# Output and down products with their weights held in the array and 512 tokens streaming, their results turned back into rows through VectorE and memory

## The reference

```python
x = x + _layernorm(attn(_layernorm(x)))      # 16 heads of 128, causal softmax, b_Q b_K b_V b_O
    out = jnp.einsum('bqhe,hed->bqd', z, W_O) + b_O
x = x + _layernorm(mlp(_layernorm(x)))       # 4-bit weights with block scales, 2048 wide
    gelu = jnp.tanh(0.7978845608028654 * (gate + 0.044715 * gate ** 3)) * gate * 0.5 + gate * 0.5
    inter = gelu * up
    out = jnp.einsum('tn,hn->th', inter, Wd)
```

## Time and profile before

| | |
|---|---|
| median of 3 runs | 1584.81 us (1583.91 to 1586.49) |
| the profiled execution, its own time | 1591.08 us |
| its span, first to last instruction | 1588.4 us |
| PE busy / weight loads | 1561.3 us (98%) / 1397.9 us (88%) |
| DVE, ACT, POOL busy | 1061.5 (67%), 974.1 (61%), 712.5 us (45%) |
| matmuls recorded | 9600 |
| granted TensorE clock, mean | 0.998 |
| DMA: bytes moved, mean rate | 167.69 MB, 106 GB/s |

### The profile page before, as it was taken

How to read it: one execution, slowest core, us unless ns; L and a number is a source line. 1 busy time by engine, 2 the same in 40 slices (tenths; PEclk the granted TensorE clock), 3 DMA queues, 4 the chain that set the end, 5 groups by cost and what they waited for, 6 DMA issues and landing times.

```text
span 1588.4 us, 28430 instructions
## 1 busy us (share of the span) xinstructions
PE 1561.3 (98%) x9600; PEld 1397.9 (88%) x9600; DVE 1061.5 (67%) x3074; ACT 974.1 (61%) x2433; POOL 712.5 (45%) x1069
## 2 busy tenths in 40 slices
PE   7999999999999999999999999999999999999998
PEld 5889898988998899889899989898888888888887
DVE  4656677677677777777767766666656565565665
ACT  5887677667776676767776767644444444444443
POOL 4674454545554455444554544333333333333333
PEclk9999999999999999999999999999999999999999
DMA  4554434443444344444443454471000011000000
GB/s 118 178 174 122 140 116 139 149 138 124 143 148 138 123 144 131 140 130 131 149 143 117 142 163 136 155 278 41 27 14 27 14 32 36 14 28 14 27 14 27
DMA packets 157440, 167.69 MB, mean 106 GB/s; under 512 B 15856, under 2 KB 130672, under 8 KB 157296
## 3 DMA queue, kind: packets, MB, share of 16 engines
q1 hardware_dynamic: 157296, 165.89, 32.9%
HBM read 94.53 MB, written 71.30 MB: 104 GB/s over the span
## 4 chain that ended last, share of the span: by engine, by line
PE 79%; DMA 6%; ACT 6%; DVE 5%; SPq 3%; issue 1%; POOL 1%; DVEq 0%; POOLq 0%
PE fbank L700 13%; PE fbank L701 13%; PE fbank L702 13%; PE obank L702 6%; PE obank L701 6%; PE obank L700 6%; PE ubank L700 5%; PE ubank L702 5%; PE ubank L701 5%; DMA turned_scratch<-turned 3%; PE ubank L724 3%; PE fbank L802 2%; DMA back<-turned_scratch 2%; SPq L498 2%; ACT probs L597 1%
## 5 line engine op out<-in xcount | busy, mean ns | idle before, releaser
L700 PE MATMUL fbank<-xnT_hi,wqk_hi 128*128 128x512 f32 x768 | 302.9, 394 | 3.7 <-POOL wqk_lo L1215 2.7
L701 PE MATMUL fbank<-xnT_lo,wqk_hi 128*128 128x512 f32 x768 | 301.3, 392 | 0.0
L702 PE MATMUL fbank<-xnT_hi,wqk_lo 128*128 128x512 f32 x768 | 300.7, 392 | 0.0
L1246 POOL TENSOR_TENSOR pT_lo<-back,pT_hi 128x512 fp32r<-128x512 f32 x128 | 166.1, 1298 | 274.3 <-ACT pT_hi L662 274.3
L608 ACT ACTIVATE w_raw<-fbank 128x512 f32<-128x512 f32 x128 | 76.5, 598 | 254.3 <-PE fbank L702 254.3
L1208 POOL TENSOR_SCALAR probs<-probs,rsum 128x128 f32<-128x128 f32 (+1 forms) x512 | 209.2, 428 | 20.7 <-DVE rsum L901 17.7
L702 PEld LDWEIGHTS fbank<-xnT_hi,wqk_lo 128*128 128x128 f32 x768 | 145.1, 189 | 31.8
L893 DVE CUSTOM_DVE_ANT_0 probs<-ubank,mask 128x128 f32<-128x128 f32 (+1 forms) x512 | 154.9, 355 | 26.4 <-PE ubank L702 26.1
L700 PEld LDWEIGHTS fbank<-xnT_hi,wqk_hi 128*128 128x128 f32 x768 | 145.2, 189 | 27.6 <-issue 2.9
L701 PEld LDWEIGHTS fbank<-xnT_lo,wqk_hi 128*128 128x128 f32 x768 | 145.3, 189 | 22.5
L982 DVE SCALAR_TENSOR_TENSOR w_raw<-w_raw,fbank 128x512 f32<-128x512 f32 x128 | 88.0, 687 | 104.0 <-ACT w_raw L608 102.2
(11 more groups left out here) (124 smaller groups left out, 4566.1 us busy)
## 6 DMA issues: line engine op xcount, KB each, us to landing
turned_scratch<-turned SPq DMA_DIRECT2D x128, 384.0 KB, 2.6
back<-turned_scratch SPq DMA_DIRECT2D x512, 96.0 KB, 2.2
w_raw<-in_w_pairs SPq DMA_DIRECT2D x32, 256.0 KB, 3.3
w_hi_scratch<-w_hi SPq DMA_DIRECT2D x48, 128.0 KB, 2.0
w_lo_scratch<-w SPq DMA_DIRECT2D x48, 128.0 KB, 2.0
x_res<-in_x SPq DMA_DIRECT2D x16, 256.0 KB, 2.9
wqk_hi<-w_hi_scratch SPq DMA_DIRECT2D x16, 256.0 KB, 4.6
wqk_lo<-w_lo_scratch SPq DMA_DIRECT2D x16, 256.0 KB, 5.0
```

The lines of the kernel that those rows point to most:

```text
L700: nc.tensor.matmul(out, a[0], b[0], start=start, stop=False, skip_group_check=skip)
L701: nc.tensor.matmul(out, a[0], b[1], start=False, stop=False, skip_group_check=skip)
L702: return nc.tensor.matmul(out, a[1], b[0], start=False, stop=stop, skip_group_check=skip)
L1246: pool.tensor_tensor(lo[:].rearrange("p u b (a j) -> p (u b) a j", j=32), mem.back[m % 2][:, :, 0:2].rearrange("p a u b j -> p (u b) a j") ...
```

## The change

The output product of a head, and the down product of a tile in MLP chunks 0 to 6, are now six matmuls of 512 columns in place of twelve of 256: 128 output columns of the weights are held, and the 512 tokens stream. The result has output columns in the partitions and tokens along the row. The down product of chunk 7 stays as it was.

To get rows again: ACT copies the result to `given` (a view of `stream`), with `b_O` as its bias in the attention, where DVE did this before (in the MLP ACT did it before too). DVE transposes it in blocks of 32, two instructions of 128x512 a chunk (`turn_given` on DVE). SP writes 512 KB to memory, waits until they have landed, and reads them back in four DMAs of 128 KB (`turn_given` on SP). Statistics and standardising (`given_stats`, `given_standard`) read the result there; `given_stats` waits for the four reads. This is done 15 times: 8 in place of the attention's results, 7 in place of the MLP's. In the attention the two transposes stand at the "sum" of steps 3 and 4, the DMAs after the `fetch` of step 5, the statistics at the "sum" of steps 6 and 8 (all at the end of step 5 before). In MLP chunk 0 the transposes stand after `gated` of tile 4, the statistics after that of tile 5, and POOL's roots move from before to after `inter_lo` of tile 4; in later chunks the transposes come at step 0, the statistics at step 2 (steps 0 and 1 before), and everything behind them one step later. `b_O` is loaded as two columns instead of a row broadcast to all partitions.

```diff
-X1_ROOTS, NEXT_ROOTS = 6, 13
+X1_ROOTS, NEXT_ROOTS = 9, 13
...
+        backs = sb("back", [P, 2, 4, 3, 2, 32])
+        self.back = [backs[:, i] for i in range(2)]
...
+        self.given = self.stream[:].rearrange("p (h a) d -> p h (a d)", h=2)
+        places = [raw, backs[:].rearrange("p n a u b j -> p (n a u b j)")[:, 0:TT * D]]
+        self.given_turned = [v.rearrange("p (a t h j) -> p a t h j", t=TT, h=2, j=BLK)
+                             for v in places]
...
+    def turn_given(n):
+
+        view = mem.given_turned[0 if n < NCH - 1 else 1]
+        sp.wait_ge(s.given, 2 * n + 2)
+        if n:
+            sp.wait_ge(s.given_back, 64 * n)
+        sp.dma_start(given_v.rearrange("k i a c -> (k i) a c"),
+                     view.rearrange("p a t h j -> p a (t h j)")).then_inc(s.given_sent, 16)
+        sp.wait_ge(s.given_sent, 16 * (n + 1))
+        for a in range(4):
+            sp.dma_start(view[32 * a:32 * a + 32].rearrange("p k t h j -> p k (t h j)"),
+                         given_v[:, :, a].rearrange("k i c -> i k c")).then_inc(s.given_back, 16)
...
         fetch(n)
+        if c and j == 5:
+            turn_given(c - 1)
...
+        turn_given(NCH - 1 + c)
         finish_y(c)
...
+        elif kind == "out" and h == HEADS - 1:
+            act.wait_ge(s.out, m // HEADS + 1)
+            for i in range(2):
+                last = act.activation(mem.given[:, i], mem.columns[i], ACT.Identity,
+                                      bias=mem.bias_o[:, i:i + 1])
+            last.then_inc(s.out_used, 1)
...
-            for t in range(TT):
-                last = three(mem.obank[t // 2][:, t % 2, :],
-                             [p[:, t * P:(t + 1) * P] for p in mem.zT],
-                             [p[:, h, :] for p in mem.wo_p],
-                             h == 0 and t % 2 == 0, h == HEADS - 1, skip=True)
+            for i in range(2):
+                last = three(mem.columns[i], [p[:, h, i * P:(i + 1) * P] for p in mem.wo_p],
+                             [p[:] for p in mem.zT], h == 0, h == HEADS - 1, skip=True)
...
+            for i in range(2) if c < NCH - 1 else ():
+                last = three(mem.columns[i], [mem.w4_at(p, k)[:, i, m % 2, :] for p in range(2)],
+                             [p for p in mem.iT[m % 4]], m == 0, m == NT - 1, skip=True)
+
+            for t in range(TT) if c == NCH - 1 else ():
...
+    def turn_given(n, i):
...
+        dve.transpose(view[:, :, :, i, :].rearrange("p a t j -> p t a j"),
+                      mem.given[:, i].rearrange("p (t a i) -> p t a i", t=TT, i=BLK)
+                      ).then_inc(s.given, 1)
+
+    def given_stats(n, t):
+        dve.wait_ge(s.given_back, 64 * (n + 1))
...
-    X1_AT = {(5, "end"): (0, 1, 2), (9, "end"): (3, 4, 5, 6)}
+    X1_AT = {(3, "sum"): (-2,), (4, "sum"): (-1,), (6, "sum"): (0,), (8, "sum"): (1, 2),
+             (9, "end"): (3, 4, 5, 6)}
...
-                last = dve.tensor_tensor(xn[:, 2 * i:2 * i + 2, :], mem.obank[i][:],
-                                         mem.bias_o[:].unsqueeze(1).broadcast_to([P, 2, D]),
-                                         ALU.add)
...
+        if c == 0:
+            for part in {4: (-1,), 5: (0, 1), 6: (2,), 7: (3,), 8: (4,), 9: (5,)}.get(m, ()):
+                finish_y(part, c)
+        else:
+            for part in {0: (-1,), 2: (0, 1), 3: (2,), 4: (3,), 5: (4,), 6: (5,)}.get(j, ()):
+                finish_y(part, c)
...
-            if m == (4 if c == 0 else 3):
+            if m == (5 if c == 0 else 4):
                 roots(y_norm(c))
```

More of the change, by code:

```diff
@@ L273, in __init__ @@
         self.obank = [bank(f"obank{i}", [P, 2, D]) for i in range(2)]
+        self.columns = [b[:].rearrange("p a d -> p (a d)") for b in self.obank]
         self.gbank = [*(self.fbank[GATES[i] % FB] for i in range(2)), self.fbank[bank_of(LAST_Z)]]
@@ L631, in scalar_program @@
         full(nth(key), mem.xnT[0][:, kt, SEQ:], mem.fbank[bank_of(key)][:, 0:SEQ]).then_inc(s.hi, 1)
-    act.wait_ge(s.bias, 64)
+    act.wait_ge(s.bias, 80)
     weights_hi(2)
@@ L692, in scalar_program @@
             for i in range(2):
-                ins = act.activation(mem.stream[:, 2 * i:2 * i + 2, :], mem.obank[i][:], ACT.Copy)
+                ins = act.activation(mem.given[:, i], mem.columns[i], ACT.Copy)
             ins.then_inc(s.down_used, 1)
@@ L918, in standardise, with given_standard @@
         return last
-    def finish_x1(part, c):
-        if part in (0, 1):
-            stats_of(xn, 2 * part)
+    def turn_given(n, i):
+        view = mem.given_turned[0 if n < NCH - 1 else 1]
+        if i == 0 and n == 0:
+            dve.wait_ge(s.w_split, len(PAIRS))
+        dve.transpose(view[:, :, :, i, :].rearrange("p a t j -> p t a j"),
[3 more added lines that the diff above has]
+        dve.wait_ge(s.given_back, 64 * (n + 1))
+        view = mem.given_turned[0 if n < NCH - 1 else 1]
+        for i in (t, t + 1):
+            last = dve.bn_stats(mem.stats[:, i, :], view[:, :, i].rearrange("p k h j -> p k (h j)"))
+        after(last)
+    def given_standard(n, t):
+        view = mem.given_turned[0 if n < NCH - 1 else 1]
+        for i in (t, t + 1):
+            last = dve.tensor_scalar(mem.stream[:, i, :].rearrange("p (h k j) -> p h k j", h=2, j=BLK),
+                                     view[:, :, i].rearrange("p k h j -> p h k j"),
+                                     mem.mv[:, i, 0:1], mem.rstd[:, i:i + 1],
+                                     ALU.subtract, ALU.mult)
+        after(last)
+    def finish_x1(part, c):
+        if part in (-2, -1):
+            dve.wait_ge(s.out_used, c)
+            turn_given(c - 1, part + 2)
+        elif part in (0, 1):
+            given_stats(c - 1, 2 * part)
         elif part == 2:
@@ L927, in finish_x1 @@
             dve.wait_ge(s.rstd, x1_norm(c))
-            after(standardise(xn, xn, 2 * (part - 3)))
+            given_standard(c - 1, 2 * (part - 3))
         else:
@@ L1067, in vector_program @@
             gated(0, 0)
-        elif kind == "out" and h == HEADS - 1:
-            dve.wait_ge(s.out, m // HEADS + 1)
-            for i in range(2):
-                last = dve.tensor_tensor(xn[:, 2 * i:2 * i + 2, :], mem.obank[i][:],
-                                         mem.bias_o[:].unsqueeze(1).broadcast_to([P, 2, D]),
-                                         ALU.add)
-            last.then_inc(s.out_used, 1)
-            dve.wait_ge(s.out_used, m // HEADS + 1)
     y = mem.stream
     def finish_y(part, c):
-        if part in (0, 1):
+        if part == -1:
             if c:
                 dve.wait_ge(s.down_used, c)
-            stats_of(y, 2 * part)
+            else:
+                dve.wait_ge(s.out_used, NCH)
+            for i in range(2):
+                turn_given(NCH - 1 + c, i)
+        elif part in (0, 1):
+            given_stats(NCH - 1 + c, 2 * part)
             if part == 1:
@@ L1088, in finish_y @@
             dve.wait_ge(s.rstd, y_norm(c))
-            after(standardise(y, y, 2 * (part - 2)))
+            given_standard(NCH - 1 + c, 2 * (part - 2))
         else:
@@ L1131, in vector_program @@
             gated(n, m)
-            if c == 0 and m < 9:
-                for part in ((0, 1) if m == 4 else (m - 3,)):
-                    finish_y(part, c)
-            else:
-                between(c, j)
+            between(c, m, j)
     for i in range(2):
```

26 lines of the change are left out of this document (14 added, 12 removed).

## The result

The changed kernel took 1594.17 us (median of 5 runs, 1591.05 to 1595.46), the kernel before beside it 1584.7 (1583.18 to 1586.49): a ratio of 1.0057, 95% interval 1.0046 to 1.0068, or 9.0 us. In a second comparison it was 1.0054 (1.0039 to 1.0068). The forecast was 1584.6 us, so the prediction was wrong: the time lies above its range.

What follows compares the result with a forecast made beforehand. PE, busy 98% of the span, was taken as the bound. Matmuls -11.5, hole +9.6, half clock +1.6, attention -2.0 and +2.1 made -0.2 us on the 1584.8 us median: 1584.6 us, range 1579 to 1591.5.

Steps and rivals of the forecast that it cites:

- The matmuls: 240 output and down products, each 1.365 us instead of 1.413: 11.5 us saved, bounds 10 to 13.
- The third rival: Output and down products: price goes by columns alone, nothing is saved and the waits remain; 1596 us, chance 0.05.
- The hole in MLP chunk 0: PE waits 9.6 us before tile 5's down product, as the write queues behind weight loads; bounds 8.4 to 12.
- The half clock: After the hole in MLP chunk 0, PE runs at 1.2 GHz for 3.13 us: 1.6 us lost, bounds 0 to 3.2.
- Attention: Attention steps 2 and 3: 2.0 us gained from DVE's relief, 2.1 us lost to a transpose ahead of `spread`; these cancel.
- the fourth rival: DVE late in attention steps 3, 4, 6 and 8: 10 us at most, about half likely, 1589.5 us; chance 0.08.
- MLP chunks 1 to 7: Later MLP chunks: the round trip through memory, 6.7 us, is just covered, so PE does not wait.
- The sum: Whole kernel: all savings and losses together come to -0.2 us, giving 1584.6 us.

Runs made afterwards that it cites:

- e11: Standalone matmul kernel, 16 x 16 pairs of held and streamed start addresses in 32-byte steps; at 512 columns 226.7 ns at remainder 0, 233.1 to 234.7 at most others.
- e12: Changed kernel with bias_o 16 columns wide instead of 2, so tiles behind it lie 32 bytes higher; 1590.48 us, 1.003 of before.
- e5: Changed kernel with zT, kT, v and the v weights allocated directly behind xnT, no instruction changed; 1589.28 us, 1.0009 of before.
- e7: Kernel of e3 with zT and v alone allocated behind xnT; 1584.47 us, 0.9984 of before.
- e3: Changed kernel with the last attention chunk's round trip through memory issued ahead of the last eight w4 weight units; 1584.88 us, 0.9982 of before.
- e8: Kernel of e3 with every tile that streams through TensorE allocated behind xnT, below 107 KB; 1580.81 us, 0.996 of before.
- e14: Changed kernel with bias_o 32 columns wide instead of 2, putting zT, kT and v at 224 past a multiple of 256 bytes; 1599.8 us in one run.
- e10: Standalone kernel, groups of 24 matmuls from thirteen SBUF regions; at 512 columns 5.44 us a group whatever the region, 5.60 with the streamed tile 32 bytes further.
- e2: Changed kernel with output products altered by chunk (streamed tile, held weights, overwriting, split); 0.227 us a matmul with xnT streaming, 0.231 to 0.235 in the other 512-column chunks.
- e4: Changed kernel with other tiles streaming through the output products; 0.227 us a matmul for q, k, v and output weights, 0.231 to 0.235 for v.

## Why the prediction was wrong, step by step

- **The matmuls: this step failed.** I had -11.5 us, with "10 to 13" as its bounds, from 0.2275 and 0.1178 us. Output products fell only from 1.413 to 1.403 us and down products from 1.411 to 1.402, 2.3 us over the 240, and gates behind a down product rose from 1.370 to 1.384, which takes back 1.6. The rows were right, but not for these operands: the 512-column matmuls of the earlier trace rows held and streamed tiles at a remainder of 0, the best for that width, and the 256-column ones were at 192, while the new products came to 32. So 0.7 came of the 11.5, and the error of 10.8 us is more than the whole miss. e11 and e12 show the cause, and e5 and e7 fit it. The third rival ("no cheaper", 1596 us, 0.05) foresaw the outcome but not the reason: the price does not go by columns alone.
- The page "TensorE: Matmul & The Clock Gate" of the Trainium skill says in Part 2 (Step-by-step: what each phase is for) that loading the next weights takes no read bandwidth in SBUF from the running matmul. By that one would not expect the place of the one tile against the other to matter; in the grid 2 to 8 ns of 227 hang on it. Whether it is the reading of the weights that costs them, no run here shows.
- **The hole in MLP chunk 0: right,** 9.6 forecast, 9.88 found, with every link: the write behind the loads, reads of 4.0 us (1065.56 to 1069.54; I had 3.6), roots ahead of the low part. e3 shows it.
- **The half clock: right in kind,** 2.8 us for 1.6, inside the bound of 3.2. The matmuls that went slow were fourteen, over 6 us, not eight over 3.13.
- **Attention: right in sum, in part by luck.** Waits before the scores of step 3 (between starts, as above) fell from 2.1 to 0.6 us, where I had -2.0 and +2.1 for the transpose. The loss came in other places: step 4 rose from 0.0 to 1.1 and step 8 from 0.9 to 2.1, and for these I had put nothing. The sum over all steps is 8.1 before and 6.9 after, so the fourth rival (DVE late by 10 us) did not come.
- **MLP chunks 1 to 7: covered,** as forecast: behind chunk 0's hole and its slow matmuls the waits are about 1 us in all, as before. In chunk 2 the reads are issued 4.3 us before DVE comes, and a read lands 2.6 us after its issue (the median of the MLP).
- **The sum.** With 2.3 less 1.6 in place of 11.5, 2.8 in place of 1.6, and 2.2 us by which q, k and v became cheaper with the new places (126 x 0.014 and 31 x 0.015, from 2.735 to 2.721 and from 5.456 to 5.441), -0.2 becomes -0.2 + 10.8 + 1.2 - 2.2 = 9.6 us; measured are 9.0 (7.3 to 10.8). The two profiled spans differ by only 5.3: that execution of before lay 6.3 us above its median, that of the changed kernel 1.3. The range was too narrow for its own terms: all bounds together reach from 1578.2 to 1592.5 us, and the bound of 10 to 13 on the matmuls allowed for an error of reading, not for a price that does not carry over.

**Open.** Why the remainder matters is not shown. Neither is why the q, k and v products of e5, e7 and e8 (and, to 2.757 and 5.477, of e14), at a remainder of 0 themselves, became dearer; in e10 twelve matmuls of 512 columns began with two to five distances of 0.228 to 0.236 us, depending on the narrow group just before, which is the same kind of thing but no rule.

## What to carry to other kernels

A duration read from one matmul holds for another only if the operands lie alike: look at the addresses of held and streamed tile as well as at the widths, and for fp32r matmuls of 512 columns keep their difference a multiple of 256 bytes. At 256 columns that was the dearest place, so the rule does not carry over to other widths without a measurement. A tile that shrinks moves everything allocated behind it, so an edit that seems to touch one operation can change the price of all. A small round trip through memory that somebody waits for is issued ahead of the bulk loads of its queue, not behind them, if the loads have time; here that was worth 10 to 12 us.

## What the runs showed of the hardware

- The distance between starts of 512-column fp32r matmuls depended on the difference of the two operands' SBUF addresses modulo 256: 226.7 ns at 0, 228.6 at 192, 233.1 to 234.7 elsewhere, at a granted clock of 1.00 (e11). SBUF region (e10), adding or overwriting (e2), and what the tile holds (e4, e5) made no difference.
- At 256 columns it lay between 113.3 and 120.1 ns, 120.0 at 0, and the remainder alone did not decide it (e11).
- After a change of pair the first distances differed by up to 10 ns from the steady ones (e10, e11, e14).
- A 512 KB write issued behind ten units of weight loads had landed, and was acted on, 11.4 us later; with eight of the ten issued behind it, 2.8 us later (e3).
- Behind a hole of 9.88 us PE's granted clock was 0.53 for 6.55 us and fourteen matmuls started 0.43 us apart, as at 1.2 GHz; behind e3's wait of 0.61 us it stayed at 1.00.
